# Second layer of a two-layer graph network: where SyncE asks for the kept counts, and whose sum stands in front of whose scaling on VectorE

## The chip, the cores and the metric

One core of one Trainium2 chip. The metric is the time of one execution on the device in microseconds (us), lower is better. Engines: TensorE (PE in the profile; PEld is its weight load), VectorE (DVE), ScalarE (ACT), GpSimd (POOL) and SyncE (SP), which only issues transfers (SPq).

## The reference, cut to what matters

```python
# first layer, with a layer norm behind it: x becomes x1 (6250 x 128)
x = _layernorm(x + _L0_gnn_ref(x, src, dst, edge_attr_128, ...))
# second layer
h = x @ W                                        # 128 x 128
src = concatenate([edge_idx[0], self_loops]); dst = concatenate([edge_idx[1], self_loops])
norm = dinv[src] * dinv[dst]                     # dinv = 1/sqrt(degree)
out = segment_sum(h[src] * norm[:, None], dst, num_segments=N) + b
y = (out - mean) * rsqrt(var + BN_EPS) * gamma + beta      # mean, var over all 6250 rows
x = _layernorm(x + where(y >= 0, y, 0.01 * y))
```

There are 6250 nodes and 200000 edges, sorted by receiver.

## The kernel before, in words

The 6250 nodes are cut into NB = 25 blocks of 256 (the last has 106). For each block the first layer builds a table of counts, "how many edges run from sender s to receiver r of this block", 128 partitions x 12800 bf16 (50 slices of 256 columns, 3200 KB), and a neighbour sum is then a product of the table with the rows of all nodes: one matmul pass for each slice and each of the high and the low half of the rows, 100 passes of 256 columns for a full sum. The tables are written to device memory (`keep_counts`, `counts_kept` in the trace), for the second layer needs the same ones.

The second layer's rows z come out of the first layer block by block. While the first layer works on block k, it already multiplies its table with those z that exist: `early(k)` passes, that is 4(k-1), at most 48. This part sum is kept in device memory (`sums_z`), and the second layer loads only the rest of the table and does the passes that are left. It takes the blocks in the order AGAIN = 0, 23, 24, 1, 2, ..., 22; i counts places in this order, b is the block. Passes left: 100 for i = 0, 52 for i = 1 and 2 (i = 2 at 112 columns), 100, 96, 92, ..., 56 for i = 3 to 14, and 52 for each of i = 15 to 24. The tables of i = 1 and 2 are still in the on-chip memory from the first layer; those of all other places are loaded into four buffers, i modulo 4 (`counts[1]`, `counts[0]` and two parts of `streams`, which hold edge data in the first layer).

For each place i the second layer does this:
- TensorE `gather_z` (L855): the passes that are left, into one of two PSUM tiles; pass q = 4b waits until GpSimd has added the node's own count (`count_itself`, L451). At the end `z_gathered` counts up.
- `add_early` on VectorE (L736): the gathered sum plus the part sum, into `s1`, of two buffers; `s1_ready` counts up. Where a block has no part sum (i = 0 and 3), ScalarE copies (`sums_out`, L1083).
- TensorE `weights` (L864): times the 128 x 128 weights; it stands behind the first 20 passes of the next place.
- VectorE `scale_rows` (L744): times dinv of the block's rows, into y; `scaled` counts up. Then ScalarE adds the bias (L1089), and VectorE takes batch-norm statistics (L729).

SyncE's queue is an order written out by hand; each request waits in it for its semaphores, and all behind it wait too:
- `load_counts(i)` (L322) waits until place i-4 is gathered (i >= 4); for i < 4 it waits for the last edge sum of the first layer (TensorE L806 of block 24).
- `load_early(i)` (L329, 128 KB) waits until the sum of place i-2 is made.
- `load_inverse(i)` (L335, dinv spread over 128 partitions, 128 KB) waits until place i-2 is scaled.

Before the change the queue runs, place by place, counts(i), early(i), inverse(i); and VectorE's order is: sum of place i+1, then scaling of place i. The first two loads, counts(0) and counts(3), stand in the loop over the first layer's blocks at b = 25, behind `keep_early(23)` (L301), which waits for ScalarE's part sum of block 23. What follows them there are the loads of the weights (L356), three vectors and dinv of places 0 and 1. Behind the last place a barrier and the final stage follow (`finish_rows`: batch norm, leaky ReLU, residual, layer norm, output).

Of the kernel before, what the change touches and what calls it, by code (L numbers as in the profile page):

```python
# [31 lines left out]
NB = -(-N // BN)  # L32
# [22 lines left out]
AGAIN = [0, NB - 2, NB - 1] + list(range(1, NB - 2))  # L55
# [26 lines left out]
def cols(b):  # L82
    return 2 * SW * slots(b)


def groups(b):
    return 2 if b < NB - 1 else -(-LAST // (EG * EC))


def edge_group(b, g):  # L90
    return 2 * b + g
# [13 lines left out]
def early(k):  # L105
    return min(4 * max(0, k - 1), EARLY_MOST)
# [23 lines left out]
def reach(engine, sem, value):  # L130


    if not isinstance(value, int) or value > 0:
        engine.wait_ge(sem, value)
# [38 lines left out]
def layers(nc, d, x, src, dst, ea, W0, b0, We, be, keep, scratch):  # L173
    with ExitStack() as ctx:
# [91 lines left out]
        def _(sp):  # L266
# [3 lines left out]
            def load_far_heads():  # L270
                sp.dma_start(heads_sb[0:1, NEAR:R].bitcast(I32), dst.rearrange("(r c) -> c r", c=HR)[0:1, NEAR:R],
                             allow_slow_non_contiguous=True).then_inc(S["heads_in"], 16)

            def start_values(b):
                sp.wait_ge(S["starts_known"], b + 1)
                return [sp.value_load(estart_i[EP * c:EP * c + 1, b:b + 1], min_val=0, max_val=E - EE)
                        for c in range(groups(b) * EG)]

            def load_destinations(b, starts):
                reach(sp, S["e_keyed"], b - 1)  # L280
                for c in range(groups(b) * EG):
                    sp.dma_start(edst[b % 2][:, c, :], dst[bass.ds(starts[c], EE)].rearrange("(p j) -> p j", j=EJ))\
                      .then_inc(edst_in[b % 2], 16)

            def load_edges(b, g, starts):
                reach(sp, S["e_summed"], edge_group(b - 1, g) + 1)
                for c in range(EG):
                    sp.dma_start(ebuf[g][:, c, :, :].rearrange("p j f -> p (j f)"),
                                 ea[bass.ds(starts[g * EG + c], EE), :].rearrange("(p j) f -> p (j f)", j=EJ))\
                      .then_inc(e_in[g], 16)  # L290

            def keep_counts(k):
                sp.wait_ge(S["pair_out"], first_slot(k) + slots(k))
                at, n = early(k) // 2 * cols(k), HI * cols(k)
                sp.dma_start(scratch["counts"][k * P:(k + 1) * P, at:n], counts[k % 2][:, at:n])\
                  .then_inc(counts_kept[k % 2], 16)

            def keep_early(k):
                sp.wait_ge(S["early_out"], early_blocks(k + 1))
                n = cols(k)  # L300
                sp.dma_start(scratch["sz"][:, k * BN:k * BN + n], early_sum[k % 2][:, 0:n]).then_inc(early_kept[k % 2], 16)  # L301

            def keep_rows(u):
                n = LAST_P if u == NB - 1 else P
                sp.wait_ge(S["x1_ready"], u + 1)
                sp.dma_start(scratch["x1"][u * BN:u * BN + 2 * n, :].rearrange("(p t) f -> p t f", t=2),
                             x1[u % 2][0:n, :, :]).then_inc(x1_kept[u % 2], 16)

            def keep_inverse(b):
                sp.wait_ge(S["shares_ready"], b + 1)  # L310
                sp.dma_start(scratch["dinv"][b * BN:b * BN + BN].rearrange("(p t) -> p t", t=2),
                             dinv[:, 2 * b:2 * b + 2]).then_inc(S["dinv_kept"], 16)

            def load_counts(i):
                b = AGAIN[i]
                at, n = early(b) // 2 * cols(b), HI * cols(b)
                if i < 4:
                    sp.wait_ge(S["e_summed"], edge_group(NB - 1, groups(NB - 1) - 1) + 1)
                else:
                    sp.wait_ge(S["z_gathered"], i - 3)  # L320
                sp.wait_ge(counts_kept[b % 2], 16 * (b // 2 + 1))
                sp.dma_start(again[AGAIN_AT[i % 4]][:, at:n], scratch["counts"][b * P:(b + 1) * P, at:n])\  # L322
                  .then_inc(counts_in[i % 4], 16)

            def load_early(i):
                b = AGAIN[i]
                reach(sp, S["s1_ready"], i - 1)
                sp.wait_ge(early_kept[b % 2], 16 * len(range(2 + b % 2, b + 1, 2)))
                sp.dma_start(early_in[i % 2][:, 0:cols(b)], scratch["sz"][:, b * BN:b * BN + cols(b)])\  # L329
                  .then_inc(early_loaded[i % 2], 16)  # L330

            def load_inverse(i):
                b = AGAIN[i]
                reach(sp, S["scaled"], i - 1)
                sp.dma_start(dinv_row[i % 2][:, :], scratch["dinv"][b * BN:(b + 1) * BN].rearrange("(o n) -> o n", o=1)  # L335
                             .to_broadcast([P, BN])).then_inc(dinv_in[i % 2], 16)
# [5 lines left out]
            for b in range(NB + 2):  # L342
                u = b - 2
                if b + 1 < NB:
                    starts = start_values(b + 1)
                    load_destinations(b + 1, starts)
                if b < NB:
                    keep_inverse(b)
                if 1 <= b <= NB - 2:
                    keep_counts(b - 1)  # L350
                if early(b - 2):
                    keep_early(b - 2)
                if b == NB:
                    load_counts(0)
                    load_counts(3)
                    sp.dma_start(w1[:, :], keep["W1"]).then_inc(S["vectors_in"], 16)  # L356
                    for k, a in enumerate(keep["vectors1"]):
                        sp.dma_start(vec[:, k:k + 1], a.rearrange("(p o) -> p o", o=1)).then_inc(S["vectors_in"], 16)
                    sp.wait_ge(S["dinv_kept"], 16 * NB)
                    for i in range(2):  # L360
                        load_inverse(i)
                if b + 1 < NB:
                    load_edges(b + 1, 0, starts)
                if 0 <= u < NB:
                    keep_rows(u)
                if b + 1 < NB and groups(b + 1) > 1:
                    load_edges(b + 1, 1, starts)
                if b == 0:
                    load_far_heads()
            for i in range(1, NB):  # L370
                if i >= 4:
                    load_counts(i)
                if early(AGAIN[i]):
                    load_early(i)
                if i >= 2:
                    load_inverse(i)
            for i in range(2):
                sp.wait_ge(early_kept[i], 16 * len(range(2 + i, NB, 2)))
                sp.wait_ge(counts_kept[i], 16 * len(range(i, NB - 2, 2)))
# [111 lines left out]
        def _(dve):  # L491
# [236 lines left out]
            def segment(k):  # L728
                dv.bn_stats(stats[:, 6 * k:6 * k + 6], y[:, SEG * k:SEG * (k + 1)]).then_inc(S["counted"], 1)  # L729

            def add_early(i):
                n = cols(AGAIN[i])
                dve.wait_ge(S["z_gathered"], i + 1)
                dve.wait_ge(early_loaded[i % 2], 16 * len([j for j in range(i % 2, i + 1, 2) if early(AGAIN[j])]))
                reach(dve, S["projected"], i - 1)
                dv.tensor_tensor(s1[i % 2][:, 0:n], z_ps[i % 2][:, 0:n], early_in[i % 2][:, 0:n], ALU.add)\  # L736
                  .then_inc(S["s1_ready"], 1)

            def scale_rows(i):
                b = AGAIN[i]  # L740
                n = cols(b)
                dve.wait_ge(S["projected"], i + 1)
                dve.wait_ge(dinv_in[i % 2], 16 * (i // 2 + 1))
                dv.tensor_tensor(y[:, b * BN:b * BN + n], y_ps[i % 2][:, 0:n], dinv_row[i % 2][:, 0:n], ALU.mult)\  # L744
                  .then_inc(S["scaled"], 1)
# [1 line left out]
            for i in range(2):  # L747
                dve.wait_ge(early_kept[i], 16 * len(range(2 + i, NB, 2)))
            for i in range(NB):
                if i + 1 < NB and early(AGAIN[i + 1]):  # L750
                    add_early(i + 1)
                scale_rows(i)
                dve.wait_ge(S["biased"], i + 1)
                if AGAIN[i] == NB - 1:
                    segment(NB - 1)
                elif AGAIN[i] < NB - 2:
                    segment(AGAIN[i])
# [829 lines left out]
```

## Time and profile before

| | |
|---|---|
| median of 3 runs | 1051.64 us (1046.19 to 1054.63) |
| profiled execution | 1049.88 us, of which the span of the trace is 1048.0 us |
| mean granted clock of TensorE | 0.968 |
| busy share of the span: PE, DVE, ACT, POOL | 88%, 66%, 45%, 34% |
| DMA, mean over the span | 237 GB/s |

The first layer fills the span up to about 748 us, the second layer's gathers stand between 748.7 and 998.3 us, and the final stage follows. All times in the rows are microseconds from the start of the span. A duration that is said to be of one matmul is of one that overlaps its neighbours; what a pass costs is the distance of starts. PEclk is the granted clock, where 1.00 is 2.4 GHz and 0.50 is 1.2 GHz.

### The profile page before, as it was taken

Reading aid. Unit: us, or ns where it says so; the run is one execution under the profiler, and the core shown is the slowest. Engines: PE = TensorE matmul, PEld = TensorE weight load, DVE = VectorE, ACT = ScalarE, POOL = GpSimd, SP = SyncE. Lnnn points to the kernel's source line nnn. Section 1 sums busy time; section 2 is a strip of 40 time slices with the busy share of each in tenths; the row PEclk is TensorE's granted clock in tenths of the full one; section 3 lists DMA queues with packets and bytes.
Section 4 is the critical chain, followed back from the end, with each engine's and each line's share of the span. In section 5 each row is a group of like instructions: output and inputs, shape, how many; then the busy total and the mean of one; then the engine's idle time right before and its main releaser. Section 6 shows DMA issues by size and latency. Waiting matters only on the chain. (4 is left out here: it accounts for less than half of the span.)

```text
span 1048.0 us, 31421 instructions
## 1 busy us (share of the span) xinstructions
PE 927.3 (88%) x12418; PEld 817.7 (78%) x12418; DVE 689.9 (66%) x1690; ACT 466.4 (45%) x944; POOL 356.5 (34%) x492
## 2 busy tenths in 40 slices
PE   1579999999999999999999999999888898687755
PEld 0467898899888888888888988899777777566655
DVE  5997999999999888788888888883110001101046
ACT  1555666666566655555555655554200000000037
POOL 4565456655544344334443342321200001111100
PEclk9989999999999999999999999999999999989888
DMA  5569989888887777667677676760755765666434
GB/s 156 185 193 341 326 315 329 303 314 310 282 296 265 265 276 265 205 236 265 194 236 233 240 266 230 228 233 17 284 194 207 266 244 185 231 217 222 161 93 156
DMA packets 95685, 247.94 MB, mean 237 GB/s; under 512 B 41128, under 2 KB 63356, under 8 KB 89644
## 3 DMA queue, kind: packets, MB, share of 16 engines
q1 hardware_dynamic: 93132, 240.97, 66.1%
q0 software_dynamic: 2400, 4.88, 1.5%
q8 instruction: 102, 1.67, 0.7%
q14 instruction: 51, 0.42, 0.1%
HBM read 185.46 MB, written 60.35 MB: 235 GB/s over the span
## 5 line engine op out<-in xcount | busy, mean ns | idle before, releaser
L950 ACT CAST counts<-pair_ps 128x800 bf16<-128x800 f32 x391 | 319.2, 829 | 278.2 <-PE pair_ps L769 274.0
L547 DVE TENSOR_TENSOR lo_oh<-counter,lo_t 128x1024 bf16<-128x1024 bf16 x391 | 274.8, 703 | 79.5 <-PE pair_ps L769 76.5
L787 PE MATMUL x_ps<-counts,xsplit 128*128 128x256 bf16 (+1 forms) x2500 | 314.8, 270 | 3.2 <-issue 1.7
L787 PEld LDWEIGHTS x_ps<-counts,xsplit 128*128 128x128 f16 x2500 | 226.3, 97 | 36.6 <-issue 14.8
L550 DVE TENSOR_TENSOR key_oh<-counter,key_t 128x800 bf16<-128x800 bf16 x391 | 231.9, 593 | 0.0
L769 PE MATMUL pair_ps<-key_oh,lo_oh 128*128 128x100 bf16 x3128 | 207.9, 209 | 25.1 <-DVE key_oh L550 18.2
L769 PEld LDWEIGHTS pair_ps<-key_oh,lo_oh 128*128 128x128 bf16 x3128 | 182.4, 98 | 41.6 <-DVE key_oh L550 22.5
L736 DVE TENSOR_TENSOR s_mem<-pair_ps,early_in 128x256 f32<-128x256 f32 (+1 forms) x23 | 9.6, 418 | 195.8 <-PE pair_ps L855 195.8
L855 PE MATMUL pair_ps<-streams,zown 128*128 128x256 bf16 x904 | 114.6, 290 | 23.3 <-DMA streams<-counts_kept 19.2
L855 PEld LDWEIGHTS pair_ps<-streams,zown 128*128 128x128 f16 x904 | 93.0, 104 | 43.3 <-DMA streams<-counts_kept 20.9
L806 PE MATMUL e_ps<-streams 128*32 128x128 f32 x3528 | 110.7, 279 | 0.8 <-issue 0.8
L1089 ACT ACTIVATE xsplit<-xsplit,vec 128x256 f32<-128x256 f32 (+1 forms) x25 | 12.6, 503 | 218.6 <-DVE xsplit L744 218.6
L855 PE MATMUL pair_ps<-counts,zown 128*128 128x256 bf16 (+1 forms) x756 | 90.6, 281 | 17.6 <-DMA counts<-counts_kept 15.7
L795 PE MATMUL x_ps<-counts,zown 128*128 128x256 bf16 (+1 forms) x840 | 103.3, 269 | 0.9 <-issue 0.9
L806 PEld LDWEIGHTS e_ps<-streams 128*32 128x32 f32 x3528 | 96.1, 112 | 6.7 <-issue 2.2
L855 PEld LDWEIGHTS pair_ps<-counts,zown 128*128 128x128 f16 x756 | 74.1, 102 | 32.9 <-DMA counts<-counts_kept 17.5
L405 POOL TENSOR_SCALAR row_f<-cnt 128x1 f32<-128x1 f32 x25 | 14.8, 590 | 208.1 <-DVE head_junk L500 207.9
L795 PEld LDWEIGHTS x_ps<-counts,zown 128*128 128x128 f16 x840 | 76.3, 97 | 11.1 <-issue 3.6
L567 DVE TENSOR_TENSOR streams<-iota,ekeys 128x1152 f32<-128x1152 f32 x49 | 66.8, 1363 | 0.0
L437 POOL TENSOR_SCALAR bias<-linear,share 128x128 f32<-128x128 f32 x50 | 53.7, 1082 | 22.9 <-DVE vo L626 22.0
L451 POOL TENSOR_TENSOR streams<-streams,key_oh 128x512 bf16<-128x512 bf16 x13 | 14.9, 1149 | 129.2 <-DMA streams<-counts_kept 129.2
L451 POOL TENSOR_TENSOR counts<-counts,key_oh 128x512 bf16<-128x512 bf16 (+1 forms) x12 | 13.2, 1106 | 94.3 <-DMA counts<-counts_kept 94.3
(158 smaller groups left out, 924.5 us busy)
## 6 DMA issues: line engine op xcount, KB each, us to landing
streams<-in_edge_attr SPq DMA_DIRECT2D x196, 576.0 KB
counts_kept<-counts SPq DMA_DIRECT2D x10, 1664.0 KB, 9.3
streams<-counts_kept SPq DMA_DIRECT2D x6, 1664.0 KB, 9.0
counts<-counts_kept SPq DMA_DIRECT2D x4, 1664.0 KB, 9.3
counts_kept<-counts SPq DMA_DIRECT2D x2, 3200.0 KB, 13.3
streams<-counts_kept SPq DMA_DIRECT2D x2, 3200.0 KB, 15.5
dinv_row<-dinv_rows SPq DMA_DIRECT2D x25, 128.0 KB, 5.1
edst<-in_dst SPq DMA_DIRECT2D x196, 4.5 KB
```

What stands on the lines that cost most here:

```text
L405: step(g.tensor_scalar(row_f[:, b:b + 1], cnt1[:, b:b + 1], float(first_head(b) - 1), 0.0, ALU.add, ALU.max))
L437: last = g.tensor_scalar(bias[:, t, :], bje, share[:, 2 * b + t:2 * b + t + 1], None, ALU.mult)
L451: g.tensor_tensor(by_hi, by_hi, itself[:, :, 0:n], ALU.add).then_inc(S["itself_counted"], 1)
L547: dv.tensor_tensor(lo_oh[:, at % RING, :, :, :], counter[:, :, :].unsqueeze(1).to_broadcast([P, SW // 2, P, 2]), pairs(lo_t[b % 2][:, w]). ...
L550: dv.tensor_tensor(key_oh[:, at % RING, :, :, :], counter[:, 0:KW, :].unsqueeze(1).to_broadcast([P, SW // 2, KW, 2]), pairs(key_t[b % 2][: ...
L567: dv.tensor_tensor(e_oh[g][:, :, :], iota[:, 0:EC].unsqueeze(1).to_broadcast([P, EG * EJ, EC]), ekeys[:, k].unsqueeze(2).to_broadcast([P, ...
L769: last = nc.tensor.matmul(pair_ps[at % 2][:, half_of, col:col + KW], lo_oh[:, at % RING, w // 2, :, w % 2], key_oh[:, at % RING, w // 2, : ...
L787: last = nc.tensor.matmul(x_ps[:, 0, 0:n], xsplit[:, q // 2, q % 2, :], by_hi[:, q // 2, :], start=(q == 0), stop=(q == 2 * HI - 1))
L795: last = nc.tensor.matmul(x_ps[:, 1, 0:n], zsplit[:, z // 2, z % 2, :], by_hi[:, z // 2, :], start=(z == 0), stop=(z == early(k) - 1))
L806: last = nc.tensor.matmul(e_ps[EC * c:EC * (c + 1), g, :], e_oh[g][:, c * EJ + j, :], ebuf[g][:, c, j, :], start=(j == 0), stop=(j == EJ - 1))
L855: last = nc.tensor.matmul(z_ps[i % 2][:, 0:n], zsplit[:, q // 2, q % 2, :], by_hi[:, q // 2, :], start=(q == early(b)), stop=(q == 2 * HI ...
L950: a.copy(out.rearrange("p h (g n) -> p h g n", g=2), pair_ps[at % 2][:, :, 0:4 * KW].rearrange("p g (n h) -> p h g n", h=HI)).then_inc(S[" ...
```

## The change

Three edits, all in the second layer:
1. counts(0) and counts(3) are asked for in iteration b = 24 of the first layer's loop, behind `keep_early(22)`, instead of b = 25.
2. In SyncE's second-layer loop, the turn of place i now asks for counts(i+3), early(i+1) and inverse(i+1) instead of counts(i), early(i), inverse(i); early(1) stands ahead of the loop. What each request waits for is unchanged.
3. On VectorE the scaling of place i stands in front of the sum of place i+1, not behind it.

```diff
-                if b == NB:
+                if b == NB - 1:
                     load_counts(0)
                     load_counts(3)
+                if b == NB:
                     sp.dma_start(w1[:, :], keep["W1"]).then_inc(S["vectors_in"], 16)
...
+            load_early(1)
             for i in range(1, NB):
-                if i >= 4:
-                    load_counts(i)
-                if early(AGAIN[i]):
-                    load_early(i)
-                if i >= 2:
-                    load_inverse(i)
+                if i + 3 < NB:
+                    load_counts(i + 3)
+                if i + 1 < NB:
+                    if early(AGAIN[i + 1]):
+                        load_early(i + 1)
+                    load_inverse(i + 1)
...
             for i in range(NB):
-                if i + 1 < NB and early(AGAIN[i + 1]):
-                    add_early(i + 1)
+                if early(AGAIN[i]):
+                    add_early(i)
                 scale_rows(i)
```

## Rows read from the trace of the kernel before

**Rows 1.** Stretches of the span: us, each engine busy (instructions), PEclk, DMA share, GB/s.
```profile
600.00:720.00 120.00, 118.29 (x1801) 107.34 (x1803) 97.88 (x212) 68.82 (x137) 41.51 (x59) 1.00 0.63 211
...
748.60:761.20 12.60, 12.51 (x102) 10.49 (x102) 0.95 (x8) 1.38 (x4) 2.77 (x3) 0.88 0.51 190
761.20:770.40 9.20, 9.20 (x111) 8.31 (x110) 1.98 (x7) 0.88 (x2) 0.00 (x0) 1.00 0.06 17
770.40:1000.00 229.60, 190.42 (x1506) 156.82 (x1502) 25.69 (x67) 11.93 (x24) 24.15 (x21) 0.91 0.62 219
```
**Rows 2.** Waits, 700 to 1010 us: who waited for whom, us, times, longest.
```profile
DVE s_mem L736 <- PE pair_ps L855: 195.8, 23, 23.1
...
PE pair_ps L855 <- DMA streams<-counts_kept: 19.2, 6, 4.2
...
PE pair_ps L855 <- DMA counts<-counts_kept: 15.7, 5, 4.0
...
PE pair_ps L855 <- POOL streams L451: 4.0, 4, 2.6
...
PE pair_ps L855 <- POOL counts L451: 1.9, 3, 0.6
```
**Rows 3.** TensorE's timeline: start, us, instructions, [idle before, releaser].
```profile
943.34 2.35 PE L855 MATMUL pair_ps<-streams,zown 128*128 128x256 bf16 x20
945.52 0.60 PE L864 MATMUL pair_ps<-s_mem,w 128*128 128x256 f32 x2
945.96 3.66 PE L855 MATMUL pair_ps<-streams,zown 128*128 128x256 bf16 x32
953.19 3.90 PE L855 MATMUL pair_ps<-streams,zown 128*128 128x256 bf16 x20 [3.58 <-DMA streams<-counts_kept]
956.93 0.60 PE L864 MATMUL pair_ps<-s_mem,w 128*128 128x256 f32 x2
957.37 3.66 PE L855 MATMUL pair_ps<-streams,zown 128*128 128x256 bf16 x32
961.09 2.36 PE L855 MATMUL pair_ps<-counts,zown 128*128 128x256 bf16 x20
```
**Rows 4.** Timeline of VectorE and SyncE in the same stretch.
```profile
943.54 0.42 DVE L736 TENSOR_TENSOR s_mem<-pair_ps,early_in 128x256 f32<-128x256 f32 x1 [10.07 <-PE pair_ps L855]
943.88 0.41 DVE L744 TENSOR_TENSOR xsplit<-pair_ps,dinv_row 128x256 f32<-128x256 f32 x1
944.32 0.32 SPq L335 DMA_DIRECT2D dinv_row<-dinv_rows  x1
...
944.73 0.38 SPq L322 DMA_DIRECT2D streams<-counts_kept  x1
...
950.85 0.38 SPq L322 DMA_DIRECT2D counts<-counts_kept  x1
```
**Rows 5.** Waits of SyncE's queue, 735 to 1010 us.
```profile
SPq L335 <- DVE xsplit L744: 187.0, 23, 15.6
```
**Rows 6.** Transfers issued from 690 to 1010 us: KB each, median us to landing.
```profile
counts<-counts_kept SPq DMA_DIRECT2D x4, 1664.0 KB, 9.3
...
dinv_row<-dinv_rows SPq DMA_DIRECT2D x25, 128.0 KB, 5.1
streams<-counts_kept SPq DMA_DIRECT2D x1, 3072.0 KB, 12.0
...
early_in<-sums_z SPq DMA_DIRECT2D x22, 128.0 KB, 9.3
```
**Rows 7.** Stretches, columns as in the first group.
```profile
739.00:743.00 4.00, 4.00 (x86) 4.00 (x83) 0.78 (x3) 1.49 (x5) 1.15 (x4) 1.00 0.99 422
...
943.30:961.10 17.80, 14.15 (x111) 11.37 (x109) 2.40 (x7) 1.01 (x2) 2.13 (x2) 0.90 0.68 222
```
**Rows 8.** Timeline where the second layer begins.
```profile
735.49 0.86 SPq L322 DMA_DIRECT2D streams<-counts_kept  x2
...
745.72 0.40 PE L838 MATMUL j_ps<-linear,se 128*128 128x128 f32 x2
...
747.40 1.15 POOL L451 TENSOR_TENSOR streams<-streams,key_oh 128x512 bf16<-128x512 bf16 x1 [7.18 <-DMA streams<-counts_kept]
...
748.69 12.48 PE L855 MATMUL pair_ps<-streams,zown 128*128 128x256 bf16 x100 [2.57 <-POOL streams L451]
...
755.33 1.15 POOL L451 TENSOR_TENSOR streams<-streams,key_oh 128x512 bf16<-128x512 bf16 x1 [5.11 <-DMA streams<-counts_kept]
```
**Rows 9.** TensorE's last edge sum, and GpSimd's last step ahead of the counts.
```profile
719.67 2.17 PE L806 MATMUL e_ps<-streams 128*32 128x128 f32 x72
...
739.63 0.58 POOL L485 CAST key_oh<-ident 128x128 bf16<-128x128 f32 x2
```
**Rows 10.** Timeline where the second layer ends.
```profile
999.06 0.70 PE L864 MATMUL pair_ps<-s_mem,w 128*128 128x256 f32 x2 [0.52 <-DVE s_mem L736]
```

## The prediction

> **What bounds the kernel now.** The page's shares (PE 88%) are an average; the chain that ended last covers only the final stage's first steps and is no help. So I read first the stretches by stage. In the first layer's late part TensorE is busy 118.29 of 120.00 us at clock 1.00; nothing is to be had there and the change doesn't touch it. In the second layer from place 3 on it is busy 190.42 of 229.60 us at 0.91 [rows 1]: 39.2 us idle, and part of what is busy runs at half clock. Then the waits: 34.9 of those 39.2 us are TensorE waiting for the loads of the counts, 5.9 for GpSimd's addition (2.6 of that before 770 us), and the longest DMA wait is 4.2 us [rows 2]. VectorE's 195.8 us of waiting for TensorE say that it is no bound, only late by its order.
>
> Why are the counts late? The timeline of one pair of places shows it. A place of 52 passes takes 2.18 us for 20 passes (943.34 to 945.52), 0.44 for the weights, and 32 passes at 2.18/20 = 0.109, 3.49 us: 6.1 us without a stall. The pair takes 17.75 us (943.34 to 961.09): TensorE has finished at 949.45, starts at 953.19, and runs its first 20 passes in 3.74 us instead of 2.18, since the clock has fallen in the gap [rows 3]. The load that it waited for was asked for only at 944.73, right behind inverse at 944.32, which followed a scaling at 943.88, which stood behind a sum that needs the end of the previous gather [rows 4]. SyncE stood 187.0 us at L335 waiting for L744, and at L322 never [rows 5]. So counts(i), whose buffer is free once place i-4 is gathered, goes out only once place i-2 is. A load of 1664 KB lands in about 9.3 us [rows 6], a place lasts 6.1, and every second place stalls.
>
> **Part 2 and 3, the loads three places ahead.** In the new order counts(i+3) waits for the end of gather i-1, which is when its buffer is free; in front of it stands inverse(i), which needs the scaling of place i-2. By the new VectorE order that scaling is made as soon as the weights of place i-2 are through, 20 passes into gather i-1; it ends some 2.18 + 0.44 + 0.41, about 3.1 us, into it, before the end of that gather. SyncE's edit carries nearly all of it: with the old VectorE order the scaling of i-2 would come 0.8 us behind the gather's end, and with the issue of inverse counts would go out 1.2 us later, 17 us of lead instead of 18. VectorE's edit alone, under the old SyncE order, would send counts 3.5 us or so sooner than now, less than the 3.7 us of idle time and 1.6 us of clock that a stall costs. Counts thus have a lead of three gathers, 3 x 6.1 = 18.3 us, against landings of 9.3 us (12.0 for 3072 KB, while a place then lasts 96 x 0.109 + 0.44 = 10.9) [rows 3, 6].
>
> What goes, in the stretch from 770.40 to the last weights at 999.06 plus 0.7 [rows 1, 10]: the passes of places 3 to 24 are 100 + (96 + 92 + ... + 56 = 836) + 10 x 52 = 1456, at 0.109 that is 158.7 us; 22 weights at 0.44 are 9.7; together 168.4 us against 229.4 now, so 61.0 us. The second working agrees: 39.2 idle, and 0.09 x 229.6 = 20.7 at the lower clock, 59.9. I take 60. Places 1 and 2 run without a stall already (9.20 busy of 9.20 us at 1.00) [rows 1].
>
> What is late next? In turn: (a) **GpSimd's addition**, 1.15 us: it waits only for the counts, which now land a place or more ahead, so its 0.6 us stalls behind the first four passes go; priced at 0, or 0.6 x 10 = 6 us if the counts land just in time. (b) **early(i+1)**, now right behind counts(i+3) in the queue: issued 0.6 us into gather i, needed at the end of gather i+1, and TensorE misses it only 2.2 us later, a lead of 2 x 6.1 - 0.6 + 1.7 = 13.3 us against 9.3 now, behind one load of counts as now [rows 6]. (c) **inverse(i+1)**: issued 3.1 us into gather i, needed 2.6 us into gather i+2, 11.7 us against 5.1. (d) **The DMA engines' throughput.** Per place 1664 + 128 + 128 KB = 1.97 MB. Two places now keep the engines busy 0.68 x 17.8 = 12.1 us, 6.05 per place; the same engines move 422 GB/s when counts alone are in flight [rows 7], by which 1.70 MB take 4.0 us and the two small loads 1.0 each. So 6.05 us of transfer stand against 6.1 us of TensorE in places 15 to 24: balanced. In places 4 to 14 TensorE is longer (96 passes 10.9 us; 3.15 MB / 422 + 2.0 = 9.5 us) and builds up the full lead. Bounds of the transfer's price: 0 if some of the small loads' time is latency that a fuller queue hides (4.7 us by 1.97 MB / 422), and upwards, if a full queue costs each place 7.5 us, 10 x 1.4 = 14 us. Nearest is the row itself, 6.05; I take 2 us for uneven landings.
>
> VectorE's edit adds no wait on the path: behind the scaling of place i, VectorE waits 0.6 us for the bias and takes statistics, all in the middle of gather i+1, which ends some 2 us later; the sum of i+1 then starts at once, as now.
>
> **Part 1, the first loads.** The last edge sum ends at 721.84, so counts(0) and (3) go out at about 722 instead of 735.49 [rows 8, 9]. The first landed 11.9 us after its issue (GpSimd starts at 747.40), the second by 755.33; now about 734 and 742. GpSimd is ready at 740.3 and has added by 741.5; TensorE's work before ends at 746.0 and the gather starts there, not at 748.69: 2.7 us. Its 100 passes took 12.48 us at a mean clock of 0.88 [rows 1] instead of 10.9; without the idle piece ahead I expect full clock, 1.5 us more (0 if the clock falls anyway). Together 4.2 us, bounds 2.7 and 4.2. Moved past them in the queue are keep_rows(22), early(23), the weights, three vectors and dinv of 0 and 1; each issue takes 0.43 us, and none of these has a reader before 748 us, so 0. The traffic meets no edge loads, since they are all in before the last edge sum. Then the last part sums land sooner as well. early(2) will follow counts(4) (12.0 us) from 757.6 and land near 769; its sum could start at 766, TensorE would miss it at 769: at most 1 us, in the 2 above.
>
> **The sum.** Profiled execution 1049.88 - 60 - 4.2 + 2 = 987.7 us. The median of the runs is 1.8 us above the profiled one: 989.4. I predict 989.
>
> **A rule weighed against the rows.** Rows: 422 GB/s into the chip's memory, held over 4 us and more [rows 7]. The Trainium skill (DMA: Bandwidth & Descriptors, Where 436 GB/s comes from) says that loads from device memory are bound at about 358 GB/s for a core. By that page counts alone would take 0.7 us more per place. The trace of this core disagrees with it, so the rule only stands beside the second rival.
>
> **Rivals.** (A) The forecast: TensorE bounds the second layer, 985 to 993. For it: every term of (a) to (d) has slack or balance. (B) **The DMA engines become the bound** in places 15 to 24: sustained, a place costs 6.8 to 7.5 us, as it would if the counts' rate were lower under three loads in flight: (0.7 to 1.4) x 10 = 7 to 14 us more, 996 to 1003, taken at 998. For it: the balance 6.05 to 6.1 leaves nothing; against: 422 GB/s with two loads in flight. The skill's page above is the rule that would give its lower end. (C) **The clock doesn't come back** with the idle time: 20 us stay, 1009. Against it: 1.00 in every stretch without a stall, with the same matmuls [rows 1]. Its kin is a change that does only half of what it says, for instance since early(i+1), issued behind counts(i+3), lands a place late; half of 60 would be 1019. (D) **Slower**: the small loads queue behind the counts of several places and set the period. With a landing of L us for early, a place lasts (L - 1.1)/2, since 0.6 us into gather i it is issued and 2 places and 1.7 us later it is missed. For places 15 to 24 to eat up what the others and the first loads gain (60 + 4 - 10 x 2.8 = 36 us), a place must last 8.9 + 3.6 = 12.5 us, so L must pass 26 us, against 9.3 now; at 30 us it is 14.5 and the time 1051.6 + 56 - 36 = 1072. For it only that several loads share the engines; against: 6.5 MB at once landed within 20 us (735.49 to 755.33) [rows 8], and early has some 3.5 MB ahead of it.
>
> **How the numbers follow.** Chances: A 0.72, B 0.17, C and its kin 0.07, within 1% 0.02, D 0.02. The range must hold 8 in 10: A and most of B, with 4 us below for a base that scatters from 1046 to 1055: 982 to 1003. One per cent is about what a measurement of this kernel can tell from no change. Faster by over 1%: 0.96; same 0.02; slower 0.02.
>
> **What would show it.** In the changed kernel's profile: L322 issues within 0.5 us of the end of each gather; SyncE's wait for L744 replaced by waits for TensorE's L855; TensorE's waits for counts near 0 and its clock 1.00 between 745 and 935; a place of 52 passes every 6.1 us; VectorE's L744 3 us into the next gather; the gather of place 0 starting at 746.0. Wrong would make me: DMA share at 1.0 with TensorE waiting for L451 or for L736 (then B), or L736 waiting for the early load (then C's kin).

## The result, and the profile after

The changed kernel takes 987.06 us (median of 4 runs, 983.99 to 991.22) against 1052.96 us for the kernel before beside it (median of 4); the ratio is 0.9388, with a 95% interval of 0.9329 to 0.9448. The profiled execution took 989.45 us with a span of 987.6 us. Of the 60.4 us between the two spans, the second layer gives nearly all; the first layer happened to run 2.7 us longer in this execution (its last edge sum ends at 724.5 instead of 721.8).

The stretches of the span, columns as in [rows 1]:
```profile
748.60:759.70 11.10, 11.10 (x104) 9.76 (x103) 2.15 (x12) 2.38 (x9) 0.00 (x0) 1.00 0.06 18
759.70:769.00 9.30, 9.30 (x112) 8.41 (x112) 2.40 (x8) 1.39 (x3) 0.00 (x0) 1.00 0.89 346
769.00:939.40 170.40, 169.23 (x1505) 149.18 (x1501) 27.65 (x66) 11.42 (x23) 24.17 (x21) 1.00 0.75 277
```
From place 3 on TensorE is busy 169.23 of 170.40 us at clock 1.00, where it was busy 190.42 of 229.60 at 0.91 [rows 1]. Both parts of the loss, idle time and half clock, are gone. These are waits from 700 to 960 us, the ones that answer to [rows 2]:
```profile
DVE s_mem L738 <- PE pair_ps L857: 74.2, 22, 6.9
...
DVE s_mem L738 <- DMA early_in<-sums_z: 3.6, 1, 3.6
...
PE pair_ps L866 <- DVE s_mem L738: 1.2, 2, 0.7
```
No wait of TensorE for counts or for GpSimd's addition is left (40.8 us before). The 1.2 us are two waits for a sum: 0.66 us at place 2, and 0.52 us behind the last gather, which stood there before too [rows 10]. TensorE's timeline in the late places, as in [rows 3]:
```profile
885.75 3.66 PE L857 MATMUL pair_ps<-streams,zown 128*128 128x256 bf16 x32
889.25 2.35 PE L857 MATMUL pair_ps<-counts,zown 128*128 128x256 bf16 x20
891.43 0.60 PE L866 MATMUL pair_ps<-s_mem,w 128*128 128x256 f32 x2
891.86 5.84 PE L857 MATMUL pair_ps<-counts,zown 128*128 128x256 bf16 x52
897.54 0.60 PE L866 MATMUL pair_ps<-s_mem,w 128*128 128x256 f32 x2
```
A place takes 6.11 us (891.43 to 897.54) and not 17.75/2 = 8.9. SyncE and VectorE in this stretch, as in [rows 4]:
```profile
883.33 0.32 SPq L322 DMA_DIRECT2D streams<-counts_kept  x1
883.34 0.42 DVE L738 TENSOR_TENSOR s_mem<-pair_ps,early_in 128x256 f32<-128x256 f32 x1 [2.07 <-PE pair_ps L857]
883.79 0.34 SPq L329 DMA_DIRECT2D early_in<-sums_z  x1
...
885.96 0.42 DVE L746 TENSOR_TENSOR xsplit<-pair_ps,dinv_row 128x256 f32<-128x256 f32 x1 [2.19 <-PE pair_ps L866]
886.41 0.32 SPq L335 DMA_DIRECT2D dinv_row<-dinv_rows  x1
```
Counts go out at the same moment as VectorE's sum starts, so at the end of a gather; the scaling comes 2.6 us later, in the middle of the next gather, and inverse follows it. SyncE's waits have moved from the scaling (187.0 us [rows 5]) to the gather itself, which is the last wait that the buffer demands:
```profile
SPq L322 <- PE pair_ps L857: 91.6, 21, 7.8
SPq L335 <- DVE xsplit L746: 49.8, 23, 2.7
```
The transfers from 690 to 955 us (KB each, median us to landing, as in [rows 6]), and the DMA engines' share in two pairs of late places (columns as above, as in [rows 7]):
```profile
counts<-counts_kept SPq DMA_DIRECT2D x4, 1664.0 KB, 6.6
...
dinv_row<-dinv_rows SPq DMA_DIRECT2D x25, 128.0 KB, 5.5
...
early_in<-sums_z SPq DMA_DIRECT2D x22, 128.0 KB, 7.1
```
```profile
879.00:891.20 12.20, 12.20 (x110) 10.77 (x108) 2.54 (x6) 1.02 (x2) 2.23 (x2) 1.00 0.87 323
891.20:903.40 12.20, 12.20 (x110) 10.76 (x109) 2.54 (x6) 1.01 (x2) 2.37 (x3) 1.00 0.90 323
```
Counts land in 6.6 us where it was 9.3, and the engines are busy 0.885 x 6.1 = 5.4 us per place, not 6.05. Last, the beginning, as in [rows 8]:
```profile
724.57 0.80 SPq L322 DMA_DIRECT2D streams<-counts_kept  x2
...
742.97 1.15 POOL L453 TENSOR_TENSOR streams<-streams,key_oh 128x512 bf16<-128x512 bf16 x1
...
748.39 0.40 PE L840 MATMUL j_ps<-linear,se 128*128 128x128 f32 x2
748.63 11.08 PE L857 MATMUL pair_ps<-streams,zown 128*128 128x256 bf16 x100
```
GpSimd has added place 0's count at 744.12, 4.5 us before TensorE needs it, and the gather follows the last message without a gap.

**One measure for what follows.** The first layer's length scatters by several us between executions (the gather of place 0 starts anywhere from 742.7 to 753.9 us in the profiles below), and the medians scatter with it. So beside each time stands the stretch of the second layer in the profile: from the start of place 0's gather to the start of the last weights. It is 999.06 - 748.69 = 250.4 us before and 938.81 - 748.63 = 190.2 us after. The scatter lies ahead of the first layer's last edge sum, which starts anywhere from 716.4 to 724.8 us; from its start to that of place 0's gather the profiles show 29.0 to 29.1 us in all kernels with the first loads at the old place and 26.3 in all with them sooner.

| kernel | second layer, us | time, us | ratio to before (95%) |
|---|---|---|---|
| before (beside the changed kernel) | 250.4 | 1052.96 | 1 |
| changed | 190.2 | 987.06 | 0.9388 (0.9329 to 0.9448) |
| first loads only | 248.9 | 1045.79 | 0.9959 (0.9921 to 0.9996) |
| VectorE's order only | 198.3 | 1001.02 | 0.9523 (0.9472 to 0.9574) |
| SyncE's order only | 191.4 | 994.37 | 0.9471 (0.9421 to 0.9521) |
| both orders, first loads as before | 191.7 | 992.13 | 0.9451 (0.9401 to 0.9500) |
| SyncE's order and first loads | 190.2 | 989.29 | 0.9422 (0.9372 to 0.9472) |
| changed, small loads at the old distance | 199.4 | 999.67 | 0.9506 (0.9450 to 0.9561) |
| changed, counts two places ahead | 189.3 | 988.05 | 0.9398 (0.9341 to 0.9454) |
| changed, small loads twice | 190.6 | 987.96 | 0.9405 (0.9351 to 0.9459) |
| changed, small loads three times | 213.8 | 1013.67 | 0.9651 (0.9577 to 0.9726) |
| changed, early ahead of counts | 189.3 | 985.13 | 0.9388 (0.9336 to 0.9440) |
| changed again | 190.0 | 986.34 | 0.9398 (0.9347 to 0.9449) |

### The profile page after: what moved, and what is told of

Its sections match the earlier page's. It is cut to its first block and busy times, and to the rows that moved or that the text cites. A ratio compares the mean times of both kernels' runs of the same rounds, so it can differ in the third digit from the quotient of the medians.

```text
span 987.6 us, 31422 instructions
## 1 busy us (share of the span) xinstructions
PE 905.9 (92%) x12418; PEld 809.5 (82%) x12418; DVE 692.1 (70%) x1690; ACT 466.2 (47%) x944; POOL 367.1 (37%) x492
## 5 line engine op out<-in xcount | busy, mean ns | idle before, releaser
L857 PE MATMUL pair_ps<-streams,zown 128*128 128x256 bf16 x904 | 101.8, 273 | 0.0
L857 PEld LDWEIGHTS pair_ps<-streams,zown 128*128 128x128 f16 x904 | 88.4, 98 | 11.5
L857 PE MATMUL pair_ps<-counts,zown 128*128 128x256 bf16 (+1 forms) x756 | 82.4, 268 | 0.0
L857 PEld LDWEIGHTS pair_ps<-counts,zown 128*128 128x128 f16 x756 | 71.6, 98 | 9.5
L439 POOL TENSOR_SCALAR bias<-linear,share 128x128 f32<-128x128 f32 x50 | 65.3, 1314 | 22.9 <-DVE vo L628 22.0
L746 DVE TENSOR_TENSOR xsplit<-pair_ps,dinv_row 128x256 f32<-128x256 f32 (+1 forms) x25 | 10.5, 419 | 58.4 <-PE pair_ps L866 57.7
```

The lines of the kernel that those rows point to most:

```text
L439: last = g.tensor_scalar(bias[:, t, :], bje, share[:, 2 * b + t:2 * b + t + 1], None, ALU.mult)
L857: last = nc.tensor.matmul(z_ps[i % 2][:, 0:n], zsplit[:, q // 2, q % 2, :], by_hi[:, q // 2, :], start=(q == early(b)), stop=(q == 2 * HI ...
```

## The experiments

### One part at a time

**SyncE's order alone.** Only edit 2 of the change:
```diff
+            load_early(1)
             for i in range(1, NB):
-                if i >= 4:
-                    load_counts(i)
...
+                if i + 3 < NB:
+                    load_counts(i + 3)
...
```


> SyncE's new order alone: counts(i+3) in turn i, VectorE's old order, first loads at the old place. My theory (the lead of the counts is what matters): inverse(i+1) goes out some 1.2 us behind the end of a gather, so counts have 17 us of lead instead of 18, the stalls of the second layer go as in the changed kernel, TensorE has no wait for counts above 1 us in total behind place 3, and only the first loads' 2.7 to 4.2 us are missing: 989 to 993 us, ratio to before 0.943. Rival (VectorE's order is needed for it, since inverse and early come late by it): TensorE waits for L736 or the counts in the places of 52 passes, 1005 us or more.

Measured: 994.37 us, 0.9471. TensorE waits 2.6 us for GpSimd at the start (the first loads), 1.1 us for two sums, and never for counts. The second layer takes 191.4 us. So the lead theory holds and the rival is out; the median lies 1.4 us above my range, and the second layer is no longer than with both orders (191.7), so that excess is not from there.

**VectorE's order alone.** Only edit 3:
```diff
-                if i + 1 < NB and early(AGAIN[i + 1]):
-                    add_early(i + 1)
+                if early(AGAIN[i]):
+                    add_early(i)
                 scale_rows(i)
```


> VectorE's new order alone, SyncE's old one. Counts then go out 3.1 us into a gather instead of 0.4 + 0.8 us behind its end, so with a landing of L us the period is the larger of 6.1 and (L + 3.1)/2. With L = 9.3 that is 6.2: by this reading of the leads VectorE's edit alone takes nearly all of the stalls as well, and the time is 991 to 997 us. Rival, as my prediction had it in a side sentence (it brings less than a stall costs): the pair pattern stays with a stall in every second place, shortened from 3.7 to some 0.5 to 1 us and with the clock falling still, 1005 to 1025 us.

Measured: 1001.02 us, 0.9523. The second layer falls from 250.4 to 198.3 us, which is 52.1 of the 58.6 us that both orders bring without the first loads. The median lies between the two ranges, 4 us above my theory's and 4 us below the rival's. TensorE's timeline in the late places (three of its five waits for counts there), and the stretch they lie in:
```profile
891.26 1.05 PE L855 MATMUL pair_ps<-streams,zown 128*128 128x256 bf16 x8 [0.65 <-DMA streams<-counts_kept]
...
905.31 2.36 PE L855 MATMUL pair_ps<-counts,zown 128*128 128x256 bf16 x20 [1.18 <-DMA counts<-counts_kept]
...
925.14 2.36 PE L855 MATMUL pair_ps<-counts,zown 128*128 128x256 bf16 x20 [0.99 <-DMA counts<-counts_kept]
```
```profile
884.00:945.00 61.00, 56.76 (x491) 48.01 (x489) 11.84 (x28) 4.57 (x9) 9.22 (x8) 1.00 0.83 290
```
Gaps of 0.65 to 1.18 us are left in about every second late place, as the rival has it, but the granted clock stays at 1.00 across them. The kernel is 9 us slower than both orders by the medians and 6.5 us by the second layer, and 5.6 us of that are idle time (4.8 for counts, 0.8 for GpSimd behind place 3). My lead formula (L + 3.1)/2 has the right form, but both of its numbers were too low. Counts land in 9.6 to 9.8 us here, and they go out behind the issue of inverse, 3.7 us into a gather and not 3.1 (the gather's start, and SyncE's issue):
```profile
884.35 2.35 PE L855 MATMUL pair_ps<-streams,zown 128*128 128x256 bf16 x20
...
888.03 0.38 SPq L322 DMA_DIRECT2D counts<-counts_kept  x1
```
(9.7 + 3.7)/2 is 6.7 us; the nine places from 884.35 to 945.41 took 6.8 each.

**The first loads alone.** Only edit 1.
```diff
-                if b == NB:
+                if b == NB - 1:
                     load_counts(0)
                     load_counts(3)
+                if b == NB:
```


> The first loads sooner, alone. My theory: the gather of place 0 starts behind TensorE's last message at once, 2.7 us sooner, at full clock, 1.4 us more: 4.2 us, ratio 0.996, and GpSimd adds its counts before 745 us. Rival: the clock falls all the same, 2.7 us, or the time is given back in places 4 and on, where the loads of the counts are late by themselves: 0.

Measured, with 10 runs: 1045.79 us, 0.9959 (0.9921 to 0.9996), so 4.3 us, from nothing to 8. The profile shows it more sharply; TensorE's timeline:
```profile
742.45 0.40 PE L839 MATMUL j_ps<-linear,se 128*128 128x128 f32 x2
742.69 3.55 PE L856 MATMUL pair_ps<-streams,zown 128*128 128x256 bf16 x31
```
The gather follows at once (2.57 us of waiting before [rows 8]), and from its start to that of the next it takes 11.1 us instead of 12.5: 2.6 + 1.4 = 4.0 us. The rival is out in both its forms: place 0's passes ran at full clock, and the second layer as a whole is 1.5 us shorter (248.9), so nothing was given back in the later places.

**Both orders without the first loads.** The changed kernel with edit 1 undone.

> SyncE's and VectorE's new orders, first loads at the old place. My theory: the changed kernel plus 4.2 us (2.7 if the clock falls anyway), 989 to 992 us, no stall behind place 3, and about the same as SyncE's order alone. Rival (the first loads matter more, since a late start costs lead in all places): more than 5 us above the changed kernel, with waits for counts in places 4 to 14.

Measured: 992.13 us, 0.9451; the second layer takes 191.7 us against 190.2, of which place 0's slower passes are 1.7 us, and the 2.6 us of waiting lie ahead of that stretch. There is no wait for counts behind place 3. The rival is out.

**The changed kernel again, and without VectorE's order.** On one chip, the second with edit 3 undone:

> The changed kernel again, as the base of the two others on the same chip: 984 to 991 us, ratio 0.939 to 0.942.

> First loads and SyncE's new order, VectorE's old order. My theory: with counts 17 us ahead the VectorE edit has nothing left to gain; inverse goes out 4 us later and still lands before its scaling; within 1 us of the changed kernel, with at most 1 us more of waits. Rival (VectorE's edit adds its share, as the gap of 2 us between SyncE's order alone and both orders without the first loads could mean): 2 to 4 us slower than the changed kernel, with a wait for it in the places of 52 passes.

Measured: 986.34 and 989.29 us, second layers of 190.0 and 190.2 us, TensorE's waits in it 1.0 and 1.2 us. The 3 us between the medians, which by themselves would fit the rival, are not in the second layer of the profiled executions, and the rival's wait in the late places is not there. The two profiles differ ahead of the last edge sum, where both kernels do the same work: it starts at 717.40 in the one and at 721.08 in the other, and place 0's gather follows 26.3 us later in both. So once SyncE asks far enough ahead, VectorE's order is worth 0.2 us or nothing in the second layer. That the medians of the pair without the first loads also favour it (992.13 against 994.37), with a second layer that is no shorter (191.7 against 191.4), is left unexplained.

### How much lead is enough

**Counts two places ahead.** The changed kernel with
```diff
-                if i + 3 < NB:
-                    load_counts(i + 3)
+                if i + 2 < NB and i + 2 >= 4:
+                    load_counts(i + 2)
```


> The changed kernel with counts(i+2) in turn i in place of counts(i+3): they go out behind inverse(i), 3.1 us into gather i-1, so with a lead of 3 x 6.1 - 3.1 = 15.2 us instead of 18.3. My theory: any lead above the landing (6.6 to 9.3 us) is as good, 985 to 991 us, no wait for counts behind place 3. Rival (the third place ahead is needed, since the DMA engines are near their limit and the full lead has to be built up): waits for counts in the late places, 995 us or more.

Measured: 988.05 us, 0.9398, second layer 189.3 us, no wait for counts. The lead is 14.6 us rather than 15.2, for counts go out 3.7 us into a gather here too (at 878.30, where the weights that stand 2.18 us into that gather start at 876.80), and it is as good as the changed kernel's 18. The wait of 0.66 us at place 2 is gone as well, which is most of the 0.9 us to the changed kernel's 190.2. Counts land in 9.7 us here:
```profile
streams<-counts_kept SPq DMA_DIRECT2D x6, 1664.0 KB, 9.7
...
dinv_row<-dinv_rows SPq DMA_DIRECT2D x21, 128.0 KB, 5.6
...
early_in<-sums_z SPq DMA_DIRECT2D x20, 128.0 KB, 6.5
```

**Small loads at the old distance.** The changed kernel with
```diff
-            load_early(1)
             for i in range(1, NB):
                 if i + 3 < NB:
                     load_counts(i + 3)
-                if i + 1 < NB:
-                    if early(AGAIN[i + 1]):
-                        load_early(i + 1)
-                    load_inverse(i + 1)
+                if early(AGAIN[i]):
+                    load_early(i)
+                if i >= 2:
+                    load_inverse(i)
```


> The changed kernel, but with early(i) and inverse(i) asked for in turn i (the old distance), behind counts(i+3). early(i) then has 6.1 - 0.4 + 1.7 = 7.4 us of lead in the places of 52 passes, against a landing of 7.1 us in the changed kernel. My theory: just enough, up to 0.5 us of waiting for L738's sum in some of the ten late places and none before, 987 to 992 us. Rival (behind the counts the small loads land as late as before the change, 9.3 us): TensorE waits 1.9 us or more for the sum in each late place, 1006 us or more.

Measured: 999.67 us, 0.9506, second layer 199.4 us. Neither expectation met it. In the late places the waits are 0.56, 0.33 and 0.15 us, as I had it. But 5.0 us come at place 1, which I had not looked at (TensorE's timeline, and the clock behind the wait):
```profile
772.72 1.22 PE L865 MATMUL pair_ps<-s_mem,w 128*128 128x256 f32 x2 [4.97 <-DVE s_mem L737]
```
```profile
767.00:772.70 5.70, 0.75 (x16) 0.58 (x12) 0.42 (x1) 0.00 (x0) 0.80 (x1) 0.82 1.01 422
772.70:777.00 4.30, 4.28 (x36) 3.86 (x37) 0.42 (x1) 0.51 (x1) 0.35 (x1) 0.50 0.91 388
```
early(1) is asked for at 760.85, 0.4 us behind counts(4) with its 3072 KB, and lands 11 us later, while place 1 lasts 6 us. The wait also costs 4.3 us at 1.2 GHz, some 2 us of work. So the sooner small loads are not needed in the steady part, but at the start they are: the line that puts early(1) ahead of the loop earns 7 of the 9.2 us.

**Early ahead of counts.** The changed kernel with
```diff
+                if i + 1 < NB and early(AGAIN[i + 1]):
+                    load_early(i + 1)
                 if i + 3 < NB:
                     load_counts(i + 3)
                 if i + 1 < NB:
-                    if early(AGAIN[i + 1]):
-                        load_early(i + 1)
                     load_inverse(i + 1)
```


> The changed kernel with early(i+1) asked for ahead of counts(i+3) in each turn. early then waits behind no counts of its own turn, counts go out 0.5 us later. My theory: TensorE's 0.66 us wait for the sum of place 2 goes, nothing else changes, early lands in 3 to 5 us instead of 7: the changed kernel less 0.7 us, no difference that can be measured. Rival (the small load right ahead slows the load of counts, as it takes 9.7 us behind inverse and 6.6 without): counts land in 9 to 10 us, which the lead of 17.8 us hides: the same time, or up to 3 us more if GpSimd's addition gets late.

Measured: 985.13 us, 0.9388, second layer 189.3 us against 190.0 for the changed kernel on the same chip. The wait at place 2 is gone, as expected; 0.7 us are too little for the medians, which can't tell the two apart. early now lands in 2.1 us (7 before), and counts in 6.6 and 7.1 us for the two buffers, so a small load of this kind right ahead does not slow them:
```profile
counts<-counts_kept SPq DMA_DIRECT2D x4, 1664.0 KB, 7.1
```

### How near the DMA engines are

The small loads are made two or three times; the copies go to memory that is free in the second layer. Only the number of copies differs between the two kernels:
```diff
-                sp.dma_start(early_in[i % 2][:, 0:cols(b)], ...)
+                for out in [early_in[i % 2][:, :]] + [spare[:, 0, i % 2, j, :] for j in range(2)]:
+                    sp.dma_start(out[:, 0:cols(b)], ...)
...
-                dve.wait_ge(early_loaded[i % 2], 16 * ...)
+                dve.wait_ge(early_loaded[i % 2], 48 * ...)
```
(and the same for `load_inverse` and `dinv_in`; for two copies, `range(1)` and 32). In both kernels the first two loads of inverse also wait until the memory for the copies is free; place 0's gather follows the last edge sum after 26.3 us all the same.

> The same with each small load made twice, 4 a place. By 0.7 us each a place of 52 passes takes 6.8 us of transfer against 6.1 of TensorE: 10 x 0.7 less the head start, 987 to 994 us. By 1.0 us each: 8.0 us a place, 1000 to 1010 us. If latency is hidden: 987 us and a DMA share below 1 throughout.

> The changed kernel with each of the two small loads made three times (the copies go to memory that nothing reads), 6 small loads a place: it measures how near the DMA engines are to being the bound. In the changed kernel's places of 52 passes they are busy 0.885 of 6.1 us, 5.4 us a place, so a small load costs (5.4 - 4.0) / 2 = 0.7 us. By that a place takes 4.0 + 6 x 0.7 = 8.2 us instead of 6.1 and those of 56 to 96 passes are 0.7 to 2.1 us longer: 36 us, less some 12 of head start: 1010 us. By the 1.0 us a small load that I read off the kernel before: 1040 to 1047 us. If most of a small load's time is latency that a full queue hides (0.3 us each by 422 GB/s): no change, 987 us.

Twice: 987.96 us, 0.9405, second layer 190.6 us. Nothing is lost, though the same stretches as above now read
```profile
879.00:891.20 12.20, 12.20 (x110) 10.76 (x109) 2.54 (x6) 1.01 (x2) 2.31 (x2) 1.00 0.99 336
891.20:903.40 12.20, 12.20 (x110) 10.76 (x109) 2.54 (x6) 1.02 (x2) 1.15 (x1) 1.00 1.02 362
```
The engines are busy all the time, at 336 and 362 GB/s, and TensorE just isn't held up. So of the three expectations the one with hidden latency has the time right, but not its share below 1. Four small loads and counts fit into 6.1 us; if counts take the 4.0 us of 422 GB/s, a small load costs at most (6.1 - 4.0)/4 = 0.5 us, an estimate by the same working that gave 0.7 for the changed kernel and 1.0 for the one before. By these estimates a small load costs less the fuller the queue is.

Three times: 1013.67 us, 0.9651, second layer 213.8 us, 23.6 more, near the 24 I had worked out (36 less some 12). But the profile does not let me keep the reason. TensorE never waits for counts; it waits 16 times for a sum, 17.3 us together, up to 2.2 us each (most of the rest is the clock, 0.96 on average from 870.6 to 950), and the sum waits for the copies of early:
```profile
DVE s_mem L742 <- DMA lo_oh<-sums_z: 91.9, 20, 7.2
...
PE pair_ps L870 <- DVE s_mem L742: 17.3, 16, 2.2
```
And SyncE's queue is nearly never waiting: of the 214 us of the second layer, only 10.1 + 6.8 + 4.0 us; its issues fill the rest (SyncE's timeline; early, inverse and counts of one turn):
```profile
911.37 0.32 SPq L331 DMA_DIRECT2D early_in<-sums_z  x1
911.74 2.66 SPq L331 DMA_DIRECT2D lo_oh<-sums_z  x2
914.44 0.44 SPq L338 DMA_DIRECT2D dinv_row<-dinv_rows  x1
914.93 1.64 SPq L338 DMA_DIRECT2D lo_oh<-dinv_rows  x2
917.29 0.32 SPq L323 DMA_DIRECT2D counts<-counts_kept  x1
```
Issues that take 0.32 us in the changed kernel take 1.3 us each in the second of these rows, and single ones elsewhere up to 5.9, while the engines' share is 0.88 from 870.6 to 950. At the shortest that each kind of issue takes here (0.32 us for the first of a load, 0.43 for a copy) the seven of a place would need 2.7 us of its 7.8, so SyncE's own work at its usual length is not the bound: something stretches the issues. Whether that is the engines, which are not full either, stays open. That the size came out right shows no more than that six small loads a place are too many and four are not.

## Why the prediction was right

The time came out at 987.06 for 989 forecast, and the terms hold one by one. That the time is met within 2 us is partly luck, since the medians move by more than that with the first layer. What the change touches is no luck: from the start of the last edge sum to the last weights the profiles show 999.06 - 719.67 = 279.4 us before and 938.81 - 722.34 = 216.5 after, 62.9 us less, where the sum had 60 + 4.2 - 2 = 62.2.

- **The stalls.** Forecast 60 us from place 1 on. Measured: from the start of place 1's gather to the last weights 999.06 - 761.22 = 237.8 us before and 938.81 - 759.76 = 179.1 after: 58.8 us. The floor was 168.4 us for places 3 to 24; without the two waits they took 938.81 - 768.94 - 0.66 - 0.52 = 168.7. The split into idle time and clock is borne out by the stretch at 1.00, so rival C is out.
- **The first loads.** Forecast 4.2, measured 4.0 in the profile of that part alone and 4.3 by its ratio; the clock did not fall, and the issues moved behind them cost nothing that shows. Place 0's gather starts at 748.63 and not at 746.0, as the signs had it, because the last edge sum came 2.7 us later in this execution.
- **What is late next.** GpSimd's waits are gone (0 taken). early does wait behind counts, as (b) said, and place 2 is the one spot where that shows: 0.66 us, at most 1 forecast. inverse has 0.8 us of waiting once, hidden. The 2 us for uneven landings were 0.66.
- **The DMA engines.** The 6.05 us of transfer per place that I set beside TensorE's 6.1 were too high: 5.4 in the changed kernel, with room for two more small loads before anything is lost. Rival B was further off than the row of before made it look: with the same loads per place, the profiles give, over six late places, 5.8 to 6.0 us of busy time a place in the three kernels that ask for counts late (before, first loads only, VectorE's order alone), and 5.4 to 5.5 in all kernels with one set of small loads and counts two or three places ahead. The likely reason, not tried by itself, is that a busy share read where the queue runs dry counts latency in with the transfers; a plan should take it as an upper bound.
- **The rule that was weighed.** By the Trainium skill (DMA: Bandwidth & Descriptors, Where 436 GB/s comes from) loads from device memory are bound at about 358 GB/s for a core. That section of the Trainium skill works the figure out as half of the 716 GB/s that two cores share, and here one core runs. The kernel with small loads twice ran at 362 GB/s for 12 us with small loads among them, and 422 GB/s stood in the kernel before [rows 7]; here the rule is not a bound, and no term needed it.

**Where it was wrong** is a side sentence with no term on it: that VectorE's edit alone would bring less than a stall costs, because it sends counts only 3.5 us sooner. It brought 52.1 us, nine tenths of both. The 3.5 us were about right: counts go out 3.7 us into a gather there and 1.4 us behind the end of one before (944.73 against 943.34 [rows 3, 4]), 3.8 us sooner. The comparison was not. I had set them against a stall of the pair, 3.7 us of idle time and 1.6 of clock, but a stall falls on every second place only: per place 1.9 + 0.8 us are lost, and 3.8 us of lead on each place cover 1.9. And the clock's part went although gaps of up to 1.18 us were left. So the gains of edits 2 and 3 are not added: 58.9 and 52.1 alone, 58.6 together (without the first loads).

## What to carry to other kernels

When a load stalls an engine in a regular pattern, compare what its issue really waits for in the queue with what its buffer demands: here the buffer was free two places earlier, and the request stood behind a small load that waited for a scaling that stood behind a sum. Any one edit that gives the load more lead than its landing takes it all, so measure such edits one at a time before keeping both. Check the start of the loop by itself: there the small loads meet the largest transfer, and the steady part says nothing about it.

## What the runs showed of the hardware

- **A short gap can keep TensorE's clock.** With VectorE's order alone, gaps of 0.65 to 1.18 us in a stretch of 61 us left the granted clock at 1.00; behind a gap of 3.58 us in the kernel before [rows 3] 20 passes took 3.74 us instead of 2.18, and behind one of 4.97 us the clock read 0.50 for 4.3 us. In between it goes either way: in the kernel with small loads three times the clock read 0.50 behind gaps of 2.04 and 2.22 us (888.4 to 890.0 and 912.3 to 914.0) and 1.00 behind 1.92, and in the kernel before it read 1.00 behind one of 2.45 us (810.2 to 813.4). So a stall that is only shortened can give back the whole of the clock's part.
- **Counts land some 3 us later right behind inverse, the load that spreads one row over 128 partitions.** Counts of 1664 KB land in 6.5 to 7.1 us in the five kernels with one set of small loads where inverse does not stand right ahead of them (changed, changed again, no first loads, small loads at the old distance, early ahead of counts), and in 8.7 to 10.2 us in the six where it does (before, first loads only, VectorE's order alone, SyncE's order alone, that with the first loads, two places ahead). early, of the same 128 KB but from 128 rows, did no such thing. With early landing in 2.1 us when it goes out ahead of counts, and inverse in 4.5 to 6.1 in the kernels where nothing goes out right ahead of it, reading the same 1 KB 128 times looks like the cause; that was not tried by itself.
